# Attention scores summed in blocks of 32 tokens and turned by VectorE's 32x32 transposition, with a new order of steps on every engine

## The reference

```
z, f, o = tanh(conv), sigmoid(conv), sigmoid(conv)      # convolution over 2 tokens
c = f * c + (1 - f) * z ;  h = o * c                    # a scan over the tokens
q, k, v, gate from layernorm(h)                         # 8 heads of 16 channels
scores[h, o, n] = q[n] . (k[n - offset_o] * (1 + scale_embed_o)) / 4 + bias[o, h]
attn = softmax over o                                   # 39 offsets: 0..32, 48, 64, 96, 128, 192, 256
h = h + (attn-weighted values * gate) @ W_out + b_out
h = h + ffn(layernorm(h))                               # top 2 of 64 experts, capacity 128, GELU
```

## Time and profile before

| | us |
|---|---|
| median of 3 runs | 429.99 (429.53 to 430.12) |
| span of the profiled execution, first to last instruction | 428.5 |
| TensorE clock granted, mean over the span | 0.997 |
| busy: PE / DVE / POOL / ACT | 405.3 / 380.8 / 372.7 / 323.1 |

### The profile page before, as it was taken

How to read it: one execution, slowest core, us unless ns; L and a number is a source line. 1 busy time by engine, 2 the same in 40 slices (tenths; PEclk the granted TensorE clock), 3 DMA queues, 4 the chain that set the end, 5 groups by cost and what they waited for, 6 DMA issues and landing times.

```text
span 428.5 us, 12683 instructions
## 1 busy us (share of the span) xinstructions
PE 405.3 (95%) x4554; PEld 278.6 (65%) x4554; DVE 380.8 (89%) x873; ACT 323.1 (75%) x728; POOL 372.7 (87%) x391
## 2 busy tenths in 40 slices
PE   8788789999999999999999999999999999998884
PEld 5444364776757676776767677676767675766763
DVE  2586999899999999999999999999999999999563
ACT  3756768879687877968687887868788796859773
POOL 7696999999989989898998989898998999997611
PEclk9999999999999999999999999999999999999998
DMA  6530866462737265372826446273735547265500
GB/s 230 192 105 2 200 165 182 105 174 62 200 88 183 79 154 150 86 207 61 198 71 149 143 120 186 55 201 82 178 95 129 158 109 190 65 182 127 133 13 24
DMA packets 78702, 56.08 MB, mean 131 GB/s; under 512 B 28304, under 2 KB 71344, under 8 KB 78512
## 3 DMA queue, kind: packets, MB, share of 16 engines
q1 hardware_dynamic: 78640, 55.28, 48.1%
HBM read 35.56 MB, written 19.70 MB: 129 GB/s over the span
## 4 chain that ended last, share of the span: by engine, by line
PE 74%; POOL 8%; issue 3%; DVE 3%; DMA 2%; ACT 1%; SPq 0%; POOLq 0%; DVEq 0%; ACTq 0%
PE bank L456 18%; PE bank L552 9%; PE bank L529 8%; PE bank L432 6%; PE bank L405 5%; PE bank L489 5%; PE bank L406 5%; PE bank L477 4%; POOL prod L1724 4%; POOL fprod L1709 3%; PE bank L468 3%; PE bank L521 2%; PE bank L505 2%; PE bank L440 2%; PE bank L424 1%
## 5 line engine op out<-in xcount | busy, mean ns | idle before, releaser
L1724 POOL TENSOR_TENSOR prod<-q,k 128x1448 f32<-128x1448 f32 (+2 forms) x48 | 145.6, 3053 | 17.4 <-ACT k L865 13.0
L1247 DVE SCALAR_TENSOR_TENSOR prod<-bank,par,k 128x1432 f32<-128x1432 f32 (+4 forms) x80 | 134.9, 1693 | 0.0
L456 PE MATMUL bank<-prod,ew 128*32 128x374 f32 (+7 forms) x1024 | 84.3, 467 | 2.4 <-ACT gate L872 1.0
L1709 POOL TENSOR_TENSOR fprod<-q,k 128x326 f32<-128x326 f32 (+6 forms) x112 | 79.0, 742 | 0.0
L456 PEld LDWEIGHTS bank<-prod,ew 128*32 128x32 f32 x1024 | 31.4, 110 | 44.9 <-issue 37.9
L972 ACT ACTIVATE hid<-bank,par 128x374 f32<-128x374 f32 x64 | 36.3, 575 | 23.8 <-PE bank L529 22.0
L799 ACT ACT_TABLE_LOAD x40 | 51.3, 1283 | 1.4 <-PEq L1944 0.7
L529 PE MATMUL bank<-x,par 128*128 128x374 f32 x128 | 48.4, 484 | 2.0 <-ACT x L925 2.0
L552 PE MATMUL bank<-par,hid 128*128 128x128 f32 x384 | 47.9, 276 | 0.0
L552 PEld LDWEIGHTS bank<-par,hid 128*128 128x128 f32 x384 | 45.9, 192 | 2.5
L405 PE MATMUL bank<-xT,par 128*128 128x374 f32 x96 | 40.9, 508 | 1.2 <-DVE mixin L1200 0.6
(11 more groups left out here) (123 smaller groups left out, 873.6 us busy)
## 6 DMA issues: line engine op xcount, KB each, us to landing
band<-band_scratch SPq DMA_DIRECT2D x16, 768.0 KB, 5.5
band_scratch<-attn SPq DMA_DIRECT2D x64, 180.4 KB, 3.0
vnear<-v_scratch SPq DMA_DIRECT2D x48, 192.0 KB, 3.1
v<-v_scratch SPq DMA_DIRECT2D x32, 192.0 KB, 4.1
v_scratch<-vtok SPq DMA_DIRECT2D x16, 192.0 KB, 3.0
xT<-x_dram SPq DMA_DIRECT2D x16, 187.5 KB, 3.4
vfar<-v_scratch SPq DMA_DIRECT2D x16, 128.0 KB, 3.3
out_dram<-osb SPq DMA_DIRECT2D x16, 128.0 KB
```

The source lines that it names most:

```text
L456: done = mm(home(f"s{c}")[32 * g:32 * g + 32, lo:N], ew[:, COLS[c] + j, :], src[:, j, lo:N], start=first or only, stop=last or only)
L1247: v.scalar_tensor_tensor(bass.AP(prod[c][:, :, :].tensor, first * N + lo, [[CW * N, 128], [N, w], [1, N - lo]]), home("q")[:, lo:N].unsque ...
L1709: last = g.tensor_tensor(fprod[:, i, o:N], q[q_.s][:, o:N], k[q_.s][:, KPAD:KPAD + N - o], ALU.mult)
L1724: g.tensor_tensor(bass.AP(prod[c][:, :, :].tensor, first * N + lo, [[CW * N, 128], [N, w], [1, N - lo]]), q[q_.s][:, lo:N].unsqueeze(1).br ...
```

## The change

`score` makes four matmuls for each offset, one for each of the four blocks of 32 tokens in a tile of 128: column group `u` holds tokens 32u to 32u+31 of each of the three tiles (at most 96 columns), and the four offsets of a step are told apart by the weights' columns (8 heads each) and add up in the same 32 rows. `scT` becomes 10 groups of 96 columns. `score_copy` adds the bias as a per-partition operand, one ACTIVATE for each group. `turn_scores` moves from PE to DVE as three 32x32 block transpositions; `score_mask` adds the masks to the first tile and to two offsets of the second. The score row has 40 cells instead of 39. The far weights and the maxima live behind the scores in bank s2, and several matmul outputs change banks. Everything is put in a new order.

```
-                        done = mm(home(f"s{c}")[32 * g:32 * g + 32, lo:N], ew[:, COLS[c] + j, :], src[:, j, lo:N],
-                                  start=first or only, stop=last or only)
+                for j in held:
+                    for u in range(CG):
+                        t0 = 0 if j == held[0] else max(0, -(-(OFFS[COLS[c] + j] - BT * (u + 1) + 1) // 128))
+                        block = bass.AP(src[:, :, :].tensor, j * NP + t0 * 128 + u * BT, [[rows * NP, 128], [128, TT - t0], [1, BT]])
+                        done = mm(home(f"s{c}")[BT * u:BT * (u + 1), at_ + t0 * BT:at_ + GW], ew[:, COLS[c] + j, :], block,
+                                  start=(j == held[0]), stop=(j == held[-1]))
...
-                lo = min(SKIP[c]) if c < CH else APART_SKIP[0]
-                A(scT[:, c, lo:N], home(f"s{c}")[:, lo:N], ACT.Copy).then_inc(scT_ready[c], 1)
+                for n in range(steps[c]):
+                    done = A(scT[:, GROUP_AT[c] + n, :], home(f"s{c}")[:, n * GW:(n + 1) * GW], ACT.Identity,
+                             bias=effb[:, GROUP_AT[c] + n:GROUP_AT[c] + n + 1])
+                done.then_inc(scT_ready[c], 1)
...
-                v.tensor_tensor(sc4[:, :, :, a:e], turned, bm[:, :, :, a:e], ALU.add).then_inc(sa_ready[c], 1)
+                blocks = scT[:, GROUP_AT[c]:GROUP_AT[c] + steps_, :].rearrange("p r (t x) -> p t r x", t=TT)
+                rows = sc[:, :, :].rearrange("p (t h) o -> p t o h", h=HEADS)[:, :, a:a + steps_ * CG, :]
+                v.transpose(rows, blocks).then_inc(sa_ready[c], 1)
+
+            def score_mask(q_):
+                for c in range(CH + 1):
+                    dve.wait_ge(sa_ready[c], q_.b + 1)
+                for t, a, e, mask in ((0, 0, NO, P("early")), (1, SPARE + 2, SPARE + 4, P("late"))):
+                    cells = sc[:, t * HEADS:(t + 1) * HEADS, a:e]
+                    done = v.tensor_tensor(cells, cells, mask.unsqueeze(1).broadcast_to([128, HEADS, e - a]), ALU.add)
+                done.then_inc(masked_ready, 1)
...
                 if a4:
-                    softmax_dense(a4)
                     softmax_far(a4)
                 if a1:
                     tanh_o(a1)
+                if a4:
+                    softmax_dense(a4)
```

More of the change, by code:

```diff
@@ L442, in value_project, with score @@
                 done.then_inc(v_mm, 1)
-            def score(q_, c, r, *before, first=False, last=False):
+            def score(q_, c, r, *before, first=False):
                 if is_first(q_) and first:
@@ L559, in turn @@
+                if a4:
+                    score(a4, 1, 0, ("g", a4), first=True)
+                    score(a4, 1, 1)
+                    score(a4, 1, 3)
+                    score(a4, 1, 2)
+                    score(a4, 0, 1, ("z", a1), ("up0", a7), first=True)
+                    score(a4, 0, 0)
+                    score(a4, 0, 2)
+                    score(a4, 0, 3)
                     score(a4, 2, 0, ("s1", a4), first=True)
-                    score(a4, 0, 3, last=True)
-                    score(a4, 2, 1, last=True)
+                    score(a4, 2, 1)
@@ L699, in _ @@
+            positions(seq[11], ("lg", seq[11]))
+            turn_h(seq[15], ("ht", seq[14]))
+            down(seq[11], 1)
+            down(seq[11], 2)
+            score(seq[14], 1, 0, ("g", seq[14]), first=True)
+            score(seq[14], 1, 1)
+            score(seq[14], 1, 3)
+            score(seq[14], 1, 2)
+            score(seq[14], 0, 0)
+            score(seq[14], 0, 2)
+            score(seq[14], 0, 3)
             score(seq[14], 2, 0, ("s1", seq[14]), first=True)
-            score(seq[14], 0, 3, last=True)
@@ L710, in _ @@
-            turn_x2(seq[12], ("ts0", seq[14]))
+            score(seq[14], 2, 1)
+            turn_band(seq[13], 2, ("pos", seq[11]))
             turn_band(seq[13], 1, ("xb", seq[15]))
-            attend(seq[13], 0, ("tb0", seq[13]), head=True)
+            project(seq[15], "k", ("dn", seq[11]), head=True)
+            project(seq[15], "q", ("tb0", seq[13]))
+            turn_x2(seq[12], ("s0", seq[14]))
+            attend(seq[13], 0, ("v", seq[14]), head=True)
             attend(seq[13], 2)
@@ L940, in softmax_far @@
                 rows = TT * HEADS
[L941 removed]
+                A(home("s2")[:, WEIGHTS:WEIGHTS + rows * NEAR].rearrange("p (o r) -> p r o", o=NEAR), sc[:, :, 0:NEAR], ACT.Exp)\
                     .then_inc(wfar_ready, 1)
@@ L1024, in turn @@
                 if a3:
-                    score_copy(a3, 1)
+                    keep_rows(a3)
+                    value_rows(a3)
+                    tanh_gate(a3)
+                if a5:
+                    norm2_ln(a5)
+                if a6:
+                    router_exp(a6)
+                if a0:
+                    tanh_f(a0)
+                if a5:
+                    norm2_exp(a5)
+                if a0:
+                    half_forget(a0)
+                if a2:
+                    norm1_ln(a2)
+                    norm1_exp(a2)
                 if a5:
                     norm2_rows(a5)
+                if a3:
+                    score_copy(a3, 1)
                 if a2:
@@ L1414, in turn @@
             def turn(at):
-                a0, a1, a2, a3, a4, a5, a6 = at(0), at(1), at(2), at(3), at(4), at(5), at(6)
+                a0, a1, a2, a3, a4, a5, a6, a7 = at(0), at(1), at(2), at(3), at(4), at(5), at(6), at(7)
+                if a7:
+                    gate_sum(a7)
                 if a4:
-                    score_add(a4, 2)
+                    turn_scores(a4, 1)
+                if a7:
+                    add_b2(a7)
+                    gate_weight(a7)
+                if a1:
+                    recur(a1)
+                if a7:
+                    finish(a7)
+                if a4:
+                    turn_scores(a4, 0)
+                    turn_scores(a4, 2)
                 if a5:
@@ L1420, in turn @@
                 if a4:
+                    score_mask(a4)
                     score_max(a4)
@@ L1589, in _ @@
             products(seq[15], 0, 3)
+            stats2(seq[13])
+            keep(seq[12])
             take_room(seq[12])
+            turn_scores(seq[15], 1)
+            add_b2(seq[12])
+            turn_scores(seq[15], 0)
             gate_sum(seq[12])
+            turn_scores(seq[15], 2)
             shift2_rows(seq[13])
-            add_b2(seq[12])
+            score_mask(seq[15])
             gate_weight(seq[12])
-            finish(seq[12])
-            score_add(seq[15], 1)
-            score_add(seq[15], 0)
-            score_add(seq[15], 2)
             score_max(seq[15])
@@ L1601, in _ @@
             softmax_sum(seq[14])
+            finish(seq[12])
             softmax_rcp(seq[14])
@@ L1706, in far_products @@
                 after(pool, p_used[CH][part], q_.b)
-                for i in range(part, LAST, LSTEPS):
+                for i in sorted(ORDER[CH][part]):
                     o = APART[i]
```

845 lines of the change are left out of this document (382 added, 463 removed).

## The result

The changed kernel takes 569.64 us, median of 4 runs (567.62 to 573.75), beside 429.8 us of the kernel before: ratio 1.3265, 95% interval 1.3212 to 1.3318. The prediction said 504 (480 to 522). The direction was right, the size was not: +17% forecast, +33% measured. Two profiled executions ran slow, 462.37 us in experiment 4 (the other three 453.1 to 456.5) and 532.59 in the last run of experiment 8 (the other three 521.9 to 525.8), so their turns are not compared with others.

A forecast was written before the change was run, and what follows sets the result against it. ACT was to replace PE as bound, 30.9 us a turn for 24.54: +57.2 in nine turns, +10.6, +6.5, +3 and -3 sum to +74.3 on 428.5, 502.8 of span, 504 us with 1.5 for the runs (480 to 522).

The forecast's parts named there:

- the two turns before the nine: From 47.09 to 93.86: 26.5 and 30.9, so 57.4 us for 46.8, the first without feed-forward steps: +10.6.
- the three turns behind them: From 314.72 to 380.04, 65.3 us before: turns of 25.8, 23.5 and 22.5 us, +6.5.
- Six loads a turn, 1283 ns, nothing hidden under them: ACT's turn: 8 table loads instead of 2, none overlapping other work, 7.70 + 0.6 = 8.3 us more.
- Waits of 2.9 us in ACT's turn: ACT waits for k and q, softmax_far, tanh_z and GELU 1: 2.9 us on 28.0 of work, a 30.9 us turn.
- It would cost nothing with ACT as bound: PE's clock: expected at 0.95 or more, and any loss of it free because ACT bounds the turn.
- Scoring 6.1 to 6.5 us: PE's scoring of a sequence: 6.1 us by columns streamed, 6.5 taken, 9.1 at most; hidden up to some 8.5.
- DVE, 1.25 us of transpositions and 0.50 of masks: DVE's turn: transpositions 1.25 us (1.2 to 2.4), masks 0.50, giving 24.1 us (25.3).
- The start, -3: Head: q and k of sequence 1 no longer wait for steps held up by POOL's far products, -3 us (0 at the other end).
- The end, +9.5 in two terms: Behind 314.72: +6.5 for three turns, and +3 behind 380.04, with two of four added loads on the last sequences' chain.
- Rival 2: Turns over 32 us from double-price transpositions, dear score copies or scoring over 8.5 us: 515 to 530; chance 0.13.
- Rival 5: ACT's table loads cost twice as much, another 1.28 us with each of the 82 added: 609; chance 0.01.
- The chain that ended last led by ACT: Predicted sign in the profile: ACT leads the chain that ended last, with the loads its largest line.

The follow-up runs named there:

- experiment 4: Mask tables copied to PSUM: on the kernel with the new scores in the old order, 454.92 us; the same edit on the changed kernel, 565.02 us.
- last run of experiment 8: Changed kernel with 42 table loads, masks in PSUM, conv z behind the value projection and the mixin ahead of shift2_rows: 525.17 us.
- experiment 1: Kernel before with three pairs of table loads added to each steady ACT turn, 8 loads a turn, nothing else: 503.65 us.
- 5: Kernel before with new scoring, transposition and masks in the old order and bank map, plus three pairs of table loads a steady turn: 534.71 us.
- experiment 7: Changed kernel with ACT's list regrouped to two table loads a turn, 527.02 us; then head and end regrouped too, 42 loads in all, 513.17 us.

## Why the prediction was wrong, by its steps

| us of span over the kernel before | head | nine turns | end | all |
|---|---|---|---|---|
| loads (experiment 1, span 503.5) | 12.6 | 55.7 | 6.7 | 75.0 |
| new scores beside them (5 less 1) | 8.9 | 10.3 | 9.5 | 28.6 |
| new order and ten more loads on top (after less 5) | 9.0 | 13.1 | 12.3 | 34.4 |

Each cell is a difference of the three marks (sequence 3's maximum at 102.04, 114.65, 123.50 and 132.53 in the four kernels; the stretch to sequence 12's 220.86, 276.59, 286.88 and 299.96).

The loads alone cost 75.0 us, which is the forecast's whole +74.3. The prediction's own terms, between the starts of the scoring of sequences 1, 3, 12 and 15:

```profile
55.09 4.82 PE L451 MATMUL bank<-prod,ew 128*32 128x96 f32 x180
118.47 2.85 PE L451 MATMUL bank<-prod,ew 128*32 128x96 f32 x128
418.43 2.85 PE L451 MATMUL bank<-prod,ew 128*32 128x96 f32 x128
504.25 4.00 PE L451 MATMUL bank<-prod,ew 128*32 128x96 f32 x183
```

| us over the kernel before | loads more | forecast | measured | missed |
|---|---|---|---|---|
| the start, to sequence 1 | 4 | -3 | +8.0 | 11.0 |
| the two turns before the nine | 10 | +10.6 | +16.6 | 6.0 |
| nine turns | 54 | +57.2 | +79.1 | 21.9 |
| the three turns behind them | 10 | +6.5 | +20.5 | 14.0 |
| the end behind 380.04 | 4 | +3 | +13.8 | 10.8 |

**The step that failed** is the one that takes all of the change but the loads and the copies to be hidden behind ACT, with "together 2.9" us of waits in its turn. In the turns the waits are 5.0 in the mean; that is a third of what was missed. The rest is in the start and the end, where no engine is the bound (behind 504.25 ACT is busy 40.5 of 62.3 us, PE 43.2) and the loads were taken to be mostly covered. The experiments put in its place: 28.6 us of new scores beside the loads (masks that wait for GpSimd, transpositions at twice their price, gaps of the fetch) and 34.4 of the new order with its ten further loads. How much of the 34.4 is each of its waits stays open.

- **Six loads a turn, 1283 ns, nothing hidden under them**: right, x122 at 1283. The overlap that each was to cost besides (0.6 us a turn) isn't seen: 19.40 + 7.70 = 27.10, measured 26.99. ACT's work in a turn, 28.0 to 29.0: right, 28.3, and the copies are 0.25 each as said (six in 1.51). ACT was to be busy 90% of a turn or more: 83% in the one shown, 85% over the nine.
- **Waits of 2.9 us in ACT's turn**: mis-sized. 3.8 with the loads alone, 5.0 in the changed kernel (5.8 in the turn shown). `tanh_z` and GELU 1 wait 3.25 instead of 1.2, the score copy 0.84 instead of nothing. k and q (1.04 for 0.8) came about as said, `softmax_far` shorter (0.35 for 0.7 to 1.1).
- **"It would cost nothing with ACT as bound"** of PE's clock: too strong, though the cost is small. ACT waits for PE's answer five times a turn, and behind a stand-still of 2.65 us PE answers at 1.2 GHz. The clock was 0.94 over the nine turns, near the 0.95 that was expected, and 0.85 behind 504.25; with 0.99 the nine turns were 5.2 us shorter.
- **Scoring 6.1 to 6.5 us**: right for instructions side by side (6.4). Missed: that it stands on a bank which the mixin frees, and the gaps of the fetch. With both it takes 9.8 us in the turn shown (253.72 to 263.48), more than the 8.5 up to which it was to be hidden. The row that set 16 ns for `attend` was 96 instructions long; 312 in a row run into the gaps. PE's turn "at the far end" is a slip: 24.54 - 0.93 + (9.1 - 5.96) is 26.8, not 27.3. Nothing hangs on it.
- **DVE, 1.25 us of transpositions and 0.50 of masks**: the transpositions take 0.92 + 0.92 + 0.54 alone, at the upper bound of 2.4, and about 1.9 by starts; masks 0.58, and 3.51 where GpSimd's products run. Alone in the old order these make DVE the bound at 25.5 us a turn.
- **The start, -3**: wrong in sign. Scoring of sequence 1 begins at 55.09 instead of 47.09. The masks' wait goes through `near_values` to PE's 5.13 us ahead of L427, and experiment 4 takes 3.0 us of it away. The rest has four loads more, and the two turns behind it have gaps without a releaser of 3.68 and 3.19 us (66.60, 82.62); that is read from the trace, not tested.
- **The end, +9.5 in two terms**: 34.3. The regrouping of experiment 7, with eight loads less there, made it 14.1 us shorter: loads that were taken to be covered weren't. How the rest divides stays open.
- **Rival 2** (over 32 us a turn) was what happened, at a price above its 515 to 530. Of the reasons it named, transpositions at double price came true, but the wait that they were to lengthen, `softmax_far`'s, is only 0.35; scoring wasn't over 8.5 us of its own, the copies weren't dear. Rival 5 (a load costs twice) is out: six loads gave 6.2 us of turn.
- **The chain that ended last led by ACT**: not decided. The page's chain after covers under a fifth of the span (PE 8%, ACT 4%, issue 4%).

No version beats the kernel before. The new scores in the old order with masks in PSUM come nearest, at 1.056.

## What to carry to other kernels

Price a change's parts by themselves: here the loads came out within 1 us in all, and what was called hidden came to nearly half of the loss. Price the head and the end like the turns: two thirds of what was missed lay there. An engine with 5 us of idle time a turn had room for 2 us of new work, as its idle time is where it waits for another engine's answer. Before a rewrite into many short instructions, count them over a turn, and look for idle rows without a releaser.

## What was not expected of the hardware

- PE stands still 0.6 to 4.0 us with no releaser where it consumes instructions at 16 to 26 ns each, at a place that follows the count of instructions: with 64 matmuls put ahead it came 64 earlier in three turns and 54 to 64 later in the next four.
- Two VectorE additions, of 320 and 16 elements, took 3.38 and 3.51 us beside GpSimd products of 3.05, the one of 16 elements alone 2.97; 0.57 for both with one input in PSUM.
- A transposition of 384 elements in blocks of 32 takes 922 ns, one of 192 takes 543; an addition of 384 with PSUM as input took 552.
- After 2.65 us without work PE ran 5.60 us at 1.2 GHz.
